# Eight-bit product stage without GpSimd: VectorE adds the bias, TensorE the residual, ScalarE copies the sum to x

## The chip, the cores and the metric

The kernel runs on one core of one Trainium2 chip. The core has a matrix engine (TensorE, PE in the profile), a vector engine (VectorE, DVE), a scalar engine (ScalarE, ACT), GpSimd (POOL), and SyncE (SP), which issues most of the transfers. Each engine takes its own instructions in order and waits on semaphores. The metric is the device time of one execution in microseconds.

## The reference, cut to what matters

The program is eight stages on x (4096 tokens of 128 values): four attentions and four feed-forward parts, each `x = x + f(layernorm(x))`. The change touches the fourth stage alone:

```
x_hat = layernorm(x).astype(bfloat16)
x_q = (x_hat.astype(float32) / s_in).astype(float8_e4m3fn)
k_q = (kernel.astype(float32) / s_k).astype(float8_e4m3fn)
y   = dot(x_q, k_q) * (s_in * s_k)          # 128 x 128 product in float32
x   = x + (y.astype(bfloat16) + bias)       # bias is bfloat16
```

## The kernel before, in words

x stays in SBUF for the whole program as 32 tiles of 128 tokens x 128 values. The eight-bit stage, `fp8_product`, treats them as 8 units of 4 tiles (`UNITS = 8`, `UNIT = 4`), so a unit is a 128x512 block. It lies at about 793 to 847 us of the profiled execution, between the attention `attn1` and the attention `attn2`; `end_of_stage` puts a barrier of all engines between stages.

The steps of a unit u, each with its line in the kernel before:

- ScalarE `normalise_unit(u)`: four ACTIVATE of one tile each (L1332), then one of 128x512 that divides by the input scale (L1340).
- VectorE `round_unit(u)`: four instructions that round to eight-bit precision (L1272, L1274, L1278, L1280).
- ScalarE `guard_unit(u)` (L1347), then VectorE `quantize_unit(u)` (L1288), which writes x_q.
- TensorE: four transposes of x_q (L1383); ScalarE `take_turned(u)` copies them from PSUM (L1354); TensorE: four products (L1389).
- ScalarE `cast_unit(u)` scales the product and rounds it to bfloat16 as y_bf (L1360).
- GpSimd adds the bias to y_bf (L1315) and then y_biased to x in place (L1319).
- VectorE `stats(u)`: four BATCH_NORM_STATS2 on the new x (L1294), which the layer norm of the next stage needs.

The order on each engine is written out in the code as a software pipeline over slots s. In slot s VectorE does round(s), stats(s-3), quantize(s-1); ScalarE does guard(s), take_turned(s-1), normalise(s+2), cast(s-1); TensorE goes unit by unit, transposes(u) and products(u); GpSimd goes unit by unit. Buffers are pairs, and so a step of unit u may also wait for unit u-2.

Before its last two stats, VectorE calculates the norm constants of the first half of the tiles (`norm_scale(FIRST_HALF)`, L197 to L212: some twenty small dependent instructions). At the end of its work TensorE does 12 `keep_warm` matmuls (L638), whose results nobody reads; the next stage's TensorE code begins with 10 more of these, and only then does it touch its own data (L1047, the first transposes of `attn2`).

Of the kernel before, what the change touches and what calls it, by code (L numbers as in the profile page):

```python
# [22 lines left out]
ALU = mybir.AluOpType  # L23
# [3 lines left out]
P = 128  # L27
# [7 lines left out]
UNIT = 4  # L35
UNITS = TILES // UNIT
# [94 lines left out]
class Core:  # L131
# [15 lines left out]
    def sb(self, name, shape, dt=F32, stack=None):  # L147
        return (stack or self.stack).enter_context(self.nc.sbuf_tensor(name, shape, dt))

    def sem(self, name):  # L150
        return self.stack.enter_context(self.nc.semaphore(name))
# [29 lines left out]
FIRST_HALF, SECOND_HALF = slice(0, HALF_TILES), slice(HALF_TILES, TILES)  # L181
# [73 lines left out]
def arrived(core, eng, *names):  # L255
    for group in names:
        eng.wait_ge(core.loaded[group], core.loads[group])
# [376 lines left out]
def keep_warm(core, bank, n):  # L634

    moving = core.w["minus_huge"][:, 0:8].rearrange("p t k -> p (t k)")
    for _ in range(n):
        core.nc.tensor.matmul(bank[:], core.w["route_lower"][:], moving, start=True, stop=True)  # L638
# [582 lines left out]
def fp8_product(core):  # L1221

    nc, w = core.nc, core.w
    with ExitStack() as stack:
        sb = lambda n, shape, dt=F32: core.sb("fp8_" + n, shape, dt, stack)
        pair = lambda n, shape, dt=F32: [sb(f"{n}{k}", shape, dt) for k in range(2)]
        sem = lambda n: core.stage_sem("fp8_" + n)
# [5 lines left out]
        ident_bf = sb("ident_bf", [P, P], BF16)  # L1233
# [3 lines left out]
        y_bf, y_biased = pair("y_bf", [P, UTOK], BF16), pair("y_biased", [P, UTOK], BF16)  # L1237
# [1 line left out]
        prepared, k_rounding, shifted = sem("prepared"), sem("k_rounding"), sem("shifted")  # L1239
        normed, valued, rounding, guarded, quantized = (sem(n) for n in ("normed", "valued", "rounding", "guarded", "quantized"))  # L1240
        xt_made, xt_taken, made_y, y_cast = sem("xt_made"), sem("xt_taken"), sem("made_y"), sem("y_cast")
        y_summed, added, stats_made = sem("y_summed"), sem("added"), sem("stats_made")
        t_bank, y_bank = core.bank[0:2], core.bank[2:4]
        t_bf = [t_bank[k][:].bitcast(BF16)[:, 0:UTOK] for k in range(2)]
        x_of = lambda u: core.x[:, u * UNIT:(u + 1) * UNIT].rearrange("p a c -> p (a c)")
        ROUND = 4

        with nc.Block() as block:

            @block.vector  # L1250
            def _(dve):
                def shifts(tiles):
                    nc.vector.scalar_tensor_tensor(shift[:, tiles], core.mean[:, tiles], -1.0, core.rstd[:, tiles],
                                                   ALU.mult, ALU.mult).then_inc(shifted, 1)

                shifts(FIRST_HALF)
                arrived(core, dve, "fp8", "ident")
                nc.vector.tensor_copy(ident_bf[:], w["ident"][:])
                nc.vector.tensor_tensor(product[:], w["fp8_scales"][:, 0:1], w["fp8_scales"][:, 1:2], ALU.mult)
                nc.vector.reciprocal(inverses[:], w["fp8_scales"][:]).then_inc(prepared, 1)  # L1260
                dve.wait_ge(prepared, 1)
                nc.vector.tensor_scalar(value[1][:, 0:P], w["fp8_kernel"][:], inverses[:, 1:2], None, ALU.mult).then_inc(prepared, 1)
                dve.wait_ge(prepared, 2)
                quantize(core, dve, k_rounding, lambda n: n, value[1][:, 0:P], (power[:, 0:P], rounded[1][:, 0:P]), kernel_q[:])
                dve.wait_ge(k_rounding, QUANTIZE_STEPS)
                norm_scale(core, dve, SECOND_HALF)
                shifts(SECOND_HALF)

                def round_unit(u):
                    v, r = value[u % 2][:], rounded[u % 2][:]  # L1270
                    dve.wait_ge(valued, u + 1)
                    nc.vector.tensor_scalar(power[:].bitcast(U32), v.bitcast(U32), 0x7F800000, None, ALU.bitwise_and).then_inc(rounding, 1)  # L1272
                    dve.wait_ge(rounding, ROUND * u + 1)
                    nc.vector.tensor_scalar(power[:], power[:], 2.0 ** -6, 1.5 * 2.0 ** 20, ALU.max, ALU.mult).then_inc(rounding, 1)  # L1274
                    dve.wait_ge(rounding, ROUND * u + 2)
                    if u >= 2:
                        dve.wait_ge(quantized, u - 1)
                    nc.vector.tensor_tensor(r, v, power[:], ALU.add).then_inc(rounding, 1)  # L1278
                    dve.wait_ge(rounding, ROUND * u + 3)
                    nc.vector.tensor_tensor(r, r, power[:], ALU.subtract).then_inc(rounding, 1)  # L1280
                    dve.wait_ge(rounding, ROUND * u + 4)

                def quantize_unit(u):
                    dve.wait_ge(guarded, u + 1)
                    if u >= 2:
                        dve.wait_ge(xt_made, u - 1)

                    nc.vector.scalar_tensor_tensor(x_q[u % 2][:], guard[u % 2][:], 0.0, rounded[u % 2][:], ALU.mult, ALU.add  # L1288
                                                   ).then_inc(quantized, 1)

                def stats(u):
                    dve.wait_ge(added, u + 1)
                    for t in range(u * UNIT, (u + 1) * UNIT):
                        ins = nc.vector.bn_stats(core.stats[:, t], core.x[:, t])  # L1294
                    ins.then_inc(stats_made, 1)

                for s in range(UNITS + 3):
                    if s == UNITS + 1:
                        dve.wait_ge(stats_made, UNITS // 2)
                        norm_scale(core, dve, FIRST_HALF)  # L1300
                    if s < UNITS:
                        round_unit(s)
                    if 0 <= s - 3:
                        stats(s - 3)
                    if 0 <= s - 1 < UNITS:
                        quantize_unit(s - 1)

            @block.gpsimd
            def _(pool):
                arrived(core, pool, "fp8")  # L1310
                for u in range(UNITS):
                    pool.wait_ge(y_cast, u + 1)
                    if u >= 2:
                        pool.wait_ge(added, u - 1)
                    nc.gpsimd.tensor_tensor(y_biased[u % 2][:].rearrange("p (t c) -> p t c", t=UNIT),  # L1315
                                            y_bf[u % 2][:].rearrange("p (t c) -> p t c", t=UNIT),
                                            w["fp8_bias"][:].unsqueeze(1).to_broadcast([P, UNIT, P]), ALU.add).then_inc(y_summed, 1)
                    pool.wait_ge(y_summed, u + 1)
                    nc.gpsimd.tensor_tensor(x_of(u), x_of(u), y_biased[u % 2][:], ALU.add).then_inc(added, 1)  # L1319

            @block.scalar
            def _(act):
# [33 lines left out]
                def cast_unit(u):  # L1356
                    act.wait_ge(made_y, u + 1)
                    if u >= 2:
                        act.wait_ge(y_summed, u - 1)
                    nc.scalar.activation(y_bf[u % 2][:], y_bank[u % 2][:], ACT.Copy, scale=product[:, 0:1]).then_inc(y_cast, 1)  # L1360

                act.wait_ge(prepared, 1)
                normalise_unit(0)
                normalise_unit(1)
                for s in range(UNITS + 2):
                    if s < UNITS:
                        guard_unit(s)
                    if 0 <= s - 1 < UNITS:
                        take_turned(s - 1)
                    if s + 2 < UNITS:  # L1370
                        normalise_unit(s + 2)
                    if 0 <= s - 1 < UNITS:
                        cast_unit(s - 1)

            @block.tensor
            def _(pe):
                pe.wait_ge(k_rounding, QUANTIZE_STEPS)
                for u in range(UNITS):
                    pe.wait_ge(quantized, u + 1)
                    if u >= 2:  # L1380
                        pe.wait_ge(xt_taken, u - 1)
                    for t in range(UNIT):
                        ins = nc.tensor.transpose(t_bf[u % 2][:, t * P:t * P + P], x_q[u % 2][:, t * P:t * P + P], ident_bf[:])  # L1383
                    ins.then_inc(xt_made, 1)
                    pe.wait_ge(xt_taken, u + 1)
                    if u >= 2:
                        pe.wait_ge(y_cast, u - 1)
                    for t in range(UNIT):
                        ins = nc.tensor.matmul(y_bank[u % 2][:, t * P:t * P + P], x_qt[u % 2][:, t * P:t * P + P], kernel_q[:],  # L1389
                                               start=True, stop=True)  # L1390
                    ins.then_inc(made_y, 1)
                arrived(core, pe, "route")
                keep_warm(core, core.bank[4], 12)


def unit_stats(core, dve, added, u):
# [1978 lines left out]
```

## Time and profile before

| what | value |
|---|---|
| median of 3 runs | 1744.29 us (1738.72 to 1745.17) |
| profiled execution: its own time | 1731.64 us |
| profiled execution: span of its instructions | 1729.8 us |
| mean granted TensorE clock over the span | 0.903 |
| busy over the span: PE, PEld, DVE, ACT, POOL | 1373.9, 1141.8, 1048.9, 920.8, 624.5 us |

The shares of the whole program say little on this stage: it takes about 54 us of 1730, and what bounds it has to be read from its own stretch. A row of a timeline gives start, duration, engine, line, operation and tiles; several equal instructions in a row are merged with xN. In brackets stands how long the engine was idle before, and who released it.

### The profile page before, as it was taken

The numbers are of one execution on the slowest core, as the hardware profiler recorded it, in microseconds if no ns is written. First come the engines' busy times: TensorE is split into PE (matmuls) and PEld (weight loads), VectorE is DVE, ScalarE is ACT, GpSimd is POOL, SyncE is SP. The second block draws the span as 40 slices with busy tenths as digits, with TensorE's granted clock in tenths as the row PEclk, the third lists the DMA queues.
The fourth block names the chain that finished last, engine by engine and source line by source line (L and its number), as shares of the span: only waits on it lengthen the run. The fifth ranks groups of instructions, "written<-read, shape, count | busy, mean of one in ns | idle before, by whom it ended". The sixth has DMA issues, their size and how long they took to land. (4 is left out here: it accounts for less than half of the span.)

```text
span 1729.8 us, 43197 instructions
## 1 busy us (share of the span) xinstructions
PE 1373.9 (79%) x16821; PEld 1141.8 (66%) x16821; DVE 1048.9 (61%) x2733; ACT 920.8 (53%) x2096; POOL 624.5 (36%) x604
## 2 busy tenths in 40 slices
PE   4799999978999998993588757777728878669893
PEld 3688888756788895872256536667725766559893
DVE  5677777753444327997899966333357878633334
ACT  2466656543454446986355325444456766326664
POOL 2332333230000003331478604777722245444442
PEclk9899999988999999995699969899968988679997
DMA  9200000029990002310000010111130000112225
GB/s 304 54 18 18 18 19 17 2 62 146 177 132 1 1 1 74 115 59 1 16 17 20 2 49 28 47 44 46 45 114 25 14 30 24 32 43 72 66 62 163
DMA packets 143529, 94.12 MB, mean 54 GB/s; under 512 B 55776, under 2 KB 130272, under 8 KB 142816
## 3 DMA queue, kind: packets, MB, share of 16 engines
q1 hardware_dynamic: 134368, 72.86, 19.6%
q0 software_dynamic: 8960, 18.50, 3.4%
q8 instruction: 136, 2.23, 0.6%
q14 instruction: 65, 0.53, 0.1%
HBM read 51.20 MB, written 40.12 MB: 53 GB/s over the span
## 5 line engine op out<-in xcount | busy, mean ns | idle before, releaser
L399 POOL TENSOR_TENSOR wide_probs<-wide_probs,wide_key_mask 128x512 f32<-128x512 f32 x64 | 82.9, 1316 | 187.2 <-ACT wide_probs L520 187.2
L1759 ACT ACTIVATE moe_hidden<-bank,moe_staged 128x128 f32<-128x128 f32 x288 | 82.2, 369 | 79.2 <-PE bank L1853 55.1
L1864 PE MATMUL bank<-moe_staged,moe_hidden 128*128 128x128 f32 x576 | 85.2, 294 | 37.2 <-ACT moe_hidden L1759 25.7
L1535 POOL DMA_INDIRECT moe_x_rows<-moe_rows,moe_source x72 | 81.3, 1129 | 77.5 <-DVE moe_source L1631 55.8
L2595 DVE TENSOR_TENSOR moe_hidden<-bank,moe_gate 128x256 f32<-128x256 f32 x104 | 44.1, 424 | 105.3 <-ACT moe_gate L2681 84.4
L1864 PEld LDWEIGHTS bank<-moe_staged,moe_hidden 128*128 128x128 f32 x576 | 75.2, 204 | 43.1 <-ACT moe_hidden L1759 29.2
L2585 POOL DMA_INDIRECT moe_results<-moe_y_rows,moe_x_rows x72 | 68.9, 958 | 90.1 <-DVE moe_y_rows L2607 65.7
L738 POOL MEMSET attn_v_bd<- 128x576 f32 x2 | 1.1, 578 | 267.6 <-POOLq L162 267.6
L768 POOL TENSOR_TENSOR attn_col_bd<-attn_col_t,group_mask_sb 128x1024 f32<-128x1024 f32 x32 | 60.7, 1898 | 86.9 <-ACT attn_row_t L969 86.9
L1541 POOL DMA_INDIRECT moe_results<-moe_y_rows,moe_dest x72 | 79.6, 1106 | 33.9 <-issue 19.0
L998 ACT ACTIVATE attn_probs<-attn_probs 128x1024 f32<-128x1024 f32 x64 | 64.2, 1049 | 50.0 <-DVE attn_probs L872 49.6
L844 DVE TENSOR_REDUCE attn_top<-bank 128x8 f32<-128x512 f32 x128 | 79.3, 682 | 18.3 <-PE bank L1030 18.3
L3029 ACT ACTIVATE moe_router<-bank,moe_rb_sb 128x512 f32<-128x512 f32 x64 | 41.4, 688 | 91.5 <-PE bank L3133 67.4
L1853 PE MATMUL bank<-moe_xb_t,moe_staged 128*128 128x128 f32 x576 | 83.5, 292 | 2.1 <-issue 1.5
L1674 DVE TENSOR_TENSOR moe_y_rows<-bank,moe_staged 128x128 f32<-128x128 f32 x72 | 20.9, 291 | 105.1 <-remote 65.0
L2731 PE MATMUL bank<-moe_xb_t,moe_staged 128*128 128x128 f32 x576 | 79.3, 281 | 0.8 <-ACT moe_xb_t L2675 0.5
L1853 PEld LDWEIGHTS bank<-moe_xb_t,moe_staged 128*128 128x128 f32 x576 | 76.1, 206 | 4.7 <-ACT moe_xb_t L1745 2.5
L872 DVE TENSOR_TENSOR attn_probs<-bank,attn_top 128x512 f32<-128x512 f32 x128 | 78.3, 675 | 0.0
L1647 DVE COPY moe_staged<-moe_pack_sb 128x1156 f32 x72 | 57.0, 793 | 31.5 <-DVE moe_y_rows L1674 18.7
L1913 POOL DMA_INDIRECT moe_rows<-moe_xhat,moe_slot x64 | 62.1, 970 | 35.9 <-issue 15.9
L2731 PEld LDWEIGHTS bank<-moe_xb_t,moe_staged 128*128 128x128 f32 x576 | 69.8, 191 | 5.1 <-ACT moe_xb_t L2675 4.7
L2681 ACT ACTIVATE moe_gate<-bank 128x256 f32<-128x256 f32 x104 | 39.8, 385 | 57.2 <-PE bank L2731 52.4
(416 smaller groups left out, 4265.2 us busy)
## 6 DMA issues: line engine op xcount, KB each, us to landing
moe_rows<-route_empty_sb SPq DMA_DIRECT2D x8, 2624.0 KB, 22.7
attn_ctx<-in_ctx_t SPq DMA_DIRECT2D x48, 128.0 KB, 2.0
moe_x_rows<-moe_rows SPq DMA_DIRECT2D x72, 66.0 KB
moe_pack_sb<-in_moe_pack SPq DMA_DIRECT2D x8, 578.0 KB, 3.9
moe_w_sb<-in_moe_w SPq DMA_DIRECT2D x2, 2048.0 KB, 10.7
moe_hot<-moe_results SPq DMA_DIRECT2D x16, 256.0 KB, 6.2
moe_y_in<-moe_results SPq DMA_DIRECT2D x16, 256.0 KB, 6.0
moe_pack_sb<-in_moe_pack SPq DMA_DIRECT2D x9, 384.0 KB, 4.3
```

Of the source, the lines that this page charges most:

```text
L399: nc.gpsimd.tensor_tensor(probs[b.parity][:, :, h2], probs[b.parity][:, :, h2], keys, ALU.mult).then_inc(masked, 1)
L844: nc.vector.tensor_reduce(top[:, j], s_bank[j][:].rearrange("p (n k) -> p n k", k=SEQ), AX, ALU.max).then_inc(topped, 1)
L872: ins = nc.vector.tensor_tensor(probs[b.parity][:, :, 4 * j:4 * j + 4], s_bank[j][:].rearrange("p (t g k) -> p t g k", t=2, k=SEQ), top[:, ...
L998: nc.scalar.activation(part, part, ACT.Exp, scale=scale).then_inc(exped, 1)
L1535: nc.gpsimd.indirect_dma_start(x_rows[s % GATHERS][:], None, rows, bass.IndirectOffsetOnAxis(ap=source[:, s:s + 1], axis=0)).then_inc(gath ...
L1541: nc.gpsimd.indirect_dma_start(results, bass.IndirectOffsetOnAxis(ap=dest[:, b:b + 1], axis=0), y_rows[b % GATHERS][:], None).then_inc(sca ...
L1759: ins = nc.scalar.activation(hidden[m % 2][:, f], hid_bank[m % 2][:, f * P:(f + 1) * P], ACT.Gelu, bias=staged[b % STAGED][:, b1_at + f:b1 ...
L1853: ins = nc.tensor.matmul(bank[m % 2][:, at:at + P], weights[:, k * P:(k + 1) * P], rhs, start=True, stop=True)
L1864: ins = nc.tensor.matmul(y_bank[m % 2][:, 0:P], hidden[m % 2][:, f], weights[:, at:at + P], start=(f == 0), stop=(f == nf - 1))
L1913: nc.gpsimd.indirect_dma_start(core.rows, bass.IndirectOffsetOnAxis(ap=self.slot[:, k, at:at + 1], axis=0), self.xhat[:, at], None).then_i ...
L2585: nc.gpsimd.indirect_dma_start(results, bass.IndirectOffsetOnAxis(ap=x_rows[b % LOADS][:, P:P + 1].bitcast(U32), axis=0), y_rows[b % GATHE ...
L2731: ins = nc.tensor.matmul(bank[m % 2][:, at:at + P], weights[:, k * P:(k + 1) * P], rhs, start=True, stop=True)
```

## The change

GpSimd has no work left in the stage. Its bias addition goes to VectorE (`bias_unit`, the same 128x512 bfloat16 operation), in slot s for unit s-2, between round(s) and stats(s-3). The residual addition goes to TensorE (`add_unit`): an identity product of x (float32, 512 columns) and an identity product of y_biased (bfloat16, 512 columns), accumulated in one of two PSUM banks. ScalarE copies the sum from PSUM to x (`take_sum`), in slot s for unit s-2, behind cast(s-1). `norm_scale(FIRST_HALF)` moves from ahead of slot 9 to the end of slot 8, and the 12 keep_warm matmuls write another bank.

```diff
@@ vector
+                def bias_unit(u):
+                    dve.wait_ge(y_cast, u + 1)
+                    if u >= 2:
+                        dve.wait_ge(summed, u - 1)
+                    nc.vector.tensor_tensor(y_biased[u % 2][:].rearrange("p (t c) -> p t c", t=UNIT),
+                                            y_bf[u % 2][:].rearrange("p (t c) -> p t c", t=UNIT),
+                                            w["fp8_bias"][:].unsqueeze(1).to_broadcast([P, UNIT, P]), ALU.add).then_inc(y_summed, 1)
+
                 for s in range(UNITS + 3):
-                    if s == UNITS + 1:
-                        dve.wait_ge(stats_made, UNITS // 2)
-                        norm_scale(core, dve, FIRST_HALF)
                     if s < UNITS:
                         round_unit(s)
+                    if 0 <= s - 2 < UNITS:
+                        bias_unit(s - 2)
                     if 0 <= s - 3:
                         stats(s - 3)
                     if 0 <= s - 1 < UNITS:
                         quantize_unit(s - 1)
-
-            @block.gpsimd
-            def _(pool):
-                arrived(core, pool, "fp8")
-                for u in range(UNITS):
-                    pool.wait_ge(y_cast, u + 1)
-                    if u >= 2:
-                        pool.wait_ge(added, u - 1)
-                    nc.gpsimd.tensor_tensor(y_biased[u % 2][:].rearrange("p (t c) -> p t c", t=UNIT),
-                                            y_bf[u % 2][:].rearrange("p (t c) -> p t c", t=UNIT),
-                                            w["fp8_bias"][:].unsqueeze(1).to_broadcast([P, UNIT, P]), ALU.add).then_inc(y_summed, 1)
-                    pool.wait_ge(y_summed, u + 1)
-                    nc.gpsimd.tensor_tensor(x_of(u), x_of(u), y_biased[u % 2][:], ALU.add).then_inc(added, 1)
+                    if s == UNITS:
+                        dve.wait_ge(stats_made, UNITS // 2)
+                        norm_scale(core, dve, FIRST_HALF)
@@ scalar
+                def take_sum(u):
+                    act.wait_ge(summed, u + 1)
+                    nc.scalar.copy(x_of(u), sum_bank[u % 2][:]).then_inc(added, 1)
+
-                for s in range(UNITS + 2):
+                for s in range(UNITS + 3):
 ...
                     if 0 <= s - 1 < UNITS:
                         cast_unit(s - 1)
+                    if 0 <= s - 2 < UNITS:
+                        take_sum(s - 2)
@@ tensor
+                def add_unit(u):
+                    pe.wait_ge(y_summed, u + 1)
+                    if u >= 2:
+                        pe.wait_ge(added, u - 1)
+                    nc.tensor.matmul(sum_bank[u % 2][:], w["ident"][:], x_of(u), start=True, stop=False)
+                    nc.tensor.matmul(sum_bank[u % 2][:], ident_bf[:], y_biased[u % 2][:], start=False, stop=True).then_inc(summed, 1)
 ...
                     ins.then_inc(made_y, 1)
+                    if u >= 1:
+                        add_unit(u - 1)
+                add_unit(UNITS - 1)
                 arrived(core, pe, "route")
-                keep_warm(core, core.bank[4], 12)
+                keep_warm(core, core.bank[6], 12)
```

The order on VectorE in a middle slot, before (round, stats, quantize; the lines are those of the kernel before):

```order
793 L1272 TENSOR_SCALAR fp_power<-fp_value 128x512
794 L1274 TENSOR_SCALAR fp_power<-fp_power 128x512
795 L1278 TENSOR_TENSOR fp_rounded<-fp_value,fp_power 128x512
796 L1280 TENSOR_TENSOR fp_rounded<-fp_rounded,fp_power 128x512
797 L1294 BN_STATS stats<-x 128x6 x4
798 L1288 SCALAR_TENSOR_TENSOR fp_x_q<-fp_guard,fp_rounded 128x512
```

And with the change (L1295 is `bias_unit`):

```order
796 L1272 TENSOR_SCALAR fp_power<-fp_value 128x512
797 L1274 TENSOR_SCALAR fp_power<-fp_power 128x512
798 L1278 TENSOR_TENSOR fp_rounded<-fp_value,fp_power 128x512
799 L1280 TENSOR_TENSOR fp_rounded<-fp_rounded,fp_power 128x512
800 L1295 TENSOR_TENSOR fp_y_biased<-fp_y_bf,fp_bias_sb 128x512
801 L1302 BN_STATS stats<-x 128x6 x4
802 L1288 SCALAR_TENSOR_TENSOR fp_x_q<-fp_guard,fp_rounded 128x512
```

The bias addition stands ahead of stats and quantize, so that both are queued behind its wait for y_bf.

The order on ScalarE in a middle slot with the change (guard, take_turned, normalise of two instructions' kinds, cast, take_sum; all but the last, L1361, stood in this order before):

```order
465 L1344 ACTIVATE fp_guard<-fp_rounded 128x512
466 L1351 COPY fp_x_qt<-bank 128x512
467 L1329 ACTIVATE fp_x_bf<-x,fp_shift,rstd 128x128 x4
468 L1337 ACTIVATE fp_value<-fp_x_bf,fp_inverses 128x512
469 L1357 ACTIVATE fp_y_bf<-bank,fp_product 128x512
470 L1361 COPY x<-bank 128x512
```

The cast stands behind the whole normalise, as it did before.

The order on TensorE of a unit with the change (transposes, products, and the two identity products of the unit ahead of it; before only the first two rows of each unit were there):

```order
1644 L1395 MATMUL bank<-fp_ident_bf,fp_x_q 128x128 x4
1645 L1401 MATMUL bank<-fp_kernel_q,fp_x_qt 128x128 x4
1646 L1387 MATMUL bank<-x,ident_sb 128x512
1647 L1388 MATMUL bank<-fp_y_biased,fp_ident_bf 128x512
```

The addition of unit u-1 is queued behind the products of unit u.

## Rows read from the trace of the kernel before

**Rows 1.** Timeline of VectorE in the stage and behind it (start, duration, instruction).
```profile
804.29 0.69 DVE L1288 SCALAR_TENSOR_TENSOR fp_x_q<-fp_guard,fp_rounded 128x512 bf16<-128x512 f32 x1
804.90 0.42 DVE L1272 TENSOR_SCALAR fp_power<-fp_value 128x512 uint32<-128x512 uint32 x1
...
807.26 0.69 DVE L1288 SCALAR_TENSOR_TENSOR fp_x_q<-fp_guard,fp_rounded 128x512 bf16<-128x512 f32 x1
...
818.09 0.87 DVE L1294 BATCH_NORM_STATS2 stats<-x 128x6 f32<-128x128 f32 x4
818.88 0.67 DVE L1288 SCALAR_TENSOR_TENSOR fp_x_q<-fp_guard,fp_rounded 128x512 bf16<-128x512 f32 x1
819.47 1.37 DVE L1272 TENSOR_SCALAR fp_power<-fp_value 128x512 uint32<-128x512 uint32 x1
...
837.33 0.67 DVE L1288 SCALAR_TENSOR_TENSOR fp_x_q<-fp_guard,fp_rounded 128x512 bf16<-128x512 f32 x1
...
845.06 1.65 DVE L1294 BATCH_NORM_STATS2 stats<-x 128x6 f32<-128x128 f32 x8
...
849.85 0.17 DVE L197 TENSOR_TENSOR mean<-stats 128x16 f32<-128x16 f32 x1
...
853.20 0.18 DVE L212 SCALAR_TENSOR_TENSOR rstd<-norm_half,rstd 128x16 f32<-128x16 f32 x1
```

**Rows 2.** All engines over the stretch of the stage (busy, instructions, granted clock).
```profile
799.00:847.00 48.00, 13.57 (x76) 7.10 (x76) 45.29 (x95) 27.37 (x54) 21.00 (x16) 0.54 0.00 1
```

**Rows 3.** Timeline of GpSimd around one stretched VectorE instruction.
```profile
819.08 1.47 POOL L1315 TENSOR_TENSOR fp_y_biased<-fp_y_bf,fp_bias_sb 128x512 bf16<-128x512 bf16 x1 [3.23 <-ACT fp_y_bf L1360]
```

**Rows 4.** Timeline of ScalarE, unit 0's cast and one whole slot.
```profile
808.54 0.67 ACT L1360 ACTIVATE fp_y_bf<-bank,fp_product 128x512 bf16<-128x512 f32 x1
...
815.55 0.58 ACT L1354 COPY fp_x_qt<-bank 128x512 bf16<-128x512 bf16 x1 [1.96 <-PE bank L1383]
816.03 1.65 ACT L1332 ACTIVATE fp_x_bf<-x,fp_shift,rstd 128x128 bf16<-128x128 f32 x4
817.71 0.72 ACT L1340 ACTIVATE fp_value<-fp_x_bf,fp_inverses 128x512 f32<-128x512 bf16 x1
818.34 0.67 ACT L1360 ACTIVATE fp_y_bf<-bank,fp_product 128x512 bf16<-128x512 f32 x1
```

**Rows 5.** ScalarE copying 128x512 float32 from PSUM in the stage before.
```profile
788.70 0.58 ACT L959 COPY attn_probs_t<-bank 128x512 f32<-128x512 f32 x1 [0.27 <-PE bank L1059]
```

**Rows 6.** Timeline of TensorE in the stage and at the next one's start.
```profile
814.90 0.61 PE L1383 MATMUL bank<-fp_ident_bf,fp_x_q 128*128 128x128 bf16 x4 [4.04 <-DVE fp_x_q L1288]
...
839.83 0.61 PE L1389 MATMUL bank<-fp_kernel_q,fp_x_qt 128*128 128x128 bf16 x4 [0.83 <-ACT fp_x_qt L1354]
840.23 4.25 PE L638 MATMUL bank<-minus_huge,route_lower_sb 128*128 128x512 bf16 x12
847.68 4.43 PE L638 MATMUL bank<-minus_huge,route_lower_sb 128*128 128x512 bf16 x10 [3.20 <-PEq L162]
851.90 0.63 PE L1047 MATMUL bank<-ident_sb,attn_xhat 128*128 128x128 f32 x2
...
859.30 0.70 PE L1086 MATMUL bank<-attn_x_t,attn_wq_sb 128*128 128x256 f32 x2 [0.46 <-ACT attn_x_t L947]
859.83 0.59 PE L1087 MATMUL bank<-attn_ctx,attn_wk_sb 128*128 128x256 f32 x2
```

**Rows 7.** TensorE alone by stretches: busy, granted clock (0.50 is half).
```profile
800.00:840.00 40.00, 9.09 (x62) 0.50 0.00 1
840.00:845.00 5.00, 4.48 (x16) 0.68 0.00 0
845.00:850.00 5.00, 2.32 (x6) 0.67 0.25 75
```

**Rows 8.** A bfloat16 TENSOR_TENSOR on VectorE elsewhere: duration ns min/median/max.
```profile
L1618 DVE TENSOR_TENSOR moe_hot<-route_iota_sb,moe_split x8: 1215/1217/1218, 1032.3 to 1046.8; 128x1024 bf16<-128x1024 bf16 x8
```

More of the change, by code:

```diff
@@ L1241, in fp8_product @@
         xt_made, xt_taken, made_y, y_cast = sem("xt_made"), sem("xt_taken"), sem("made_y"), sem("y_cast")
-        y_summed, added, stats_made = sem("y_summed"), sem("added"), sem("stats_made")
-        t_bank, y_bank = core.bank[0:2], core.bank[2:4]
+        y_summed, summed, added, stats_made = sem("y_summed"), sem("summed"), sem("added"), sem("stats_made")
+        t_bank, y_bank, sum_bank = core.bank[0:2], core.bank[2:4], core.bank[4:6]
         t_bf = [t_bank[k][:].bitcast(BF16)[:, 0:UTOK] for k in range(2)]
@@ L1373, in _ @@
                         cast_unit(s - 1)
+                    if 0 <= s - 2 < UNITS:
+                        take_sum(s - 2)
             @block.tensor
             def _(pe):
+                arrived(core, pe, "ident")
                 pe.wait_ge(k_rounding, QUANTIZE_STEPS)
+                def add_unit(u):
[4 more added lines that the diff above has]
+                    nc.tensor.matmul(sum_bank[u % 2][:], ident_bf[:], y_biased[u % 2][:], start=False, stop=True).then_inc(summed, 1)
                 for u in range(UNITS):
```

## The prediction, made before the changed kernel ran

> **What bounds the stage now.** I read the stage's own stretch first, then the timelines of its engines side by side. Over 799 to 847 us VectorE is busy 45.29 of 48 us and GpSimd 21.00 [rows 2], so VectorE sets the pace, and GpSimd's work is hidden beside it. The reader should then look at VectorE's durations. A unit of rounding starts at 804.90 and its quantize at 807.26 [rows 1]: 2.36 us for four instructions while GpSimd is idle. The same L1272 takes 1.37 us at 819.47 in place of 0.42, while GpSimd does its bias addition at 819.08 to 820.55 [rows 1, 3]. Two things on VectorE are not stretched: the four statistics (0.87 us) and a quantize that meets no GpSimd work (0.67 us). The pace of before: the first quantize ends at 804.98, the last (of eight) at 838.00, so 7 steps in 33.02 us, 4.72 each; in the middle, where GpSimd works in each unit, about 5.3. TensorE is busy 9.09 of 40 us at half clock [rows 7] and ScalarE has waits of about 2 us in a slot [rows 4].
>
> **What the change removes.** GpSimd's 16 instructions lie beside VectorE's work, so their own time counts only at the tail, and what disappears is the stretching of VectorE. Without it a slot of VectorE would cost, start to start: rounding 2.36, statistics 0.79 (818.09 to 818.88), quantize 0.59 (818.88 to 819.47) [rows 1]. The bias addition is new on VectorE. The nearest row of the same length is the quantize at 807.26, 0.69 us for 128x512 from two tensors to bfloat16 [rows 1]; the nearest bfloat16 row, L1618, takes 1.217 us for 1024 elements, which is the same price per element [rows 8]. I take 0.69 (0.60 start to start); half of the elements' part, 0.42, is the lower bound, by L1272's row of a faster form of the same length. The sum is 4.34 us, less than 4.72. If VectorE never waited, the stage would be shorter.
>
> The Trainium skill (VectorE: DVE Perf Modes, "The perf-mode tier table") says that a tensor_tensor whose tensors are all bfloat16 runs at two elements a cycle; L1618's row [rows 8] shows one, though its second operand is spread along the innermost dimension and the bias is not. By the page the addition would take about 0.42 us by estimate, by the row 0.69. It is behind a wait and beside a longer path in all slots but the first, so the sum would differ by 0.3 us.
>
> **What it adds: a wait in front of quantize.** The bias addition of unit s-1 comes in slot s+1, right behind rounding, and waits for ScalarE's cast of the same unit; statistics and quantize are queued behind it. I follow one slot from T, the end of quantize(s-1), with durations and gaps of [rows 1, 4, 6]:
>
> - TensorE's transposes start at T+0.06 and end at T+0.67 (814.90, 0.61).
> - ScalarE's take_turned runs T+0.71 to 1.29, and normalise begins 0.48 behind its start; from there to the start of the cast it is 2.31 us (816.03 to 818.34), so the cast starts at T+3.50 and ends at T+4.17.
> - VectorE has ended its rounding at T+2.3 and stands still for 1.9 us. The bias addition runs T+4.21 to 4.90.
> - The statistics wait for take_sum(s-2), which ScalarE does behind that cast, from T+4.07 at the earliest. It needs the sum from TensorE. The products start at T+1.35, and the next matmul can start 0.40 later (839.83 to 840.23), at T+1.75. At full clock a 256-column float32 product (two rows in the trace) takes 0.53 us until the next starts (859.30 to 859.83). Twice the columns at half the clock is at most 4 x 0.53 = 2.12, where the loading of the weights, which does not grow with the columns, is counted twice too often. The lower end is 4 times a bfloat16 product of 512 columns (4.22 us for ten keep_warm at half clock, 0.42 each), 1.69, since 0.53 for 256 columns is 5 times that product's price per column, loading included. I take 1.9. The bfloat16 product adds 0.63 until its result is there (its own streaming 0.43, drain 0.2). The sum is ready at T+1.75+1.9+0.63 = T+4.28.
> - take_sum, at L959's 0.58 [rows 5], runs T+4.32 to 4.90 (0.67 as the cast would be the upper bound). Statistics start at T+4.94, quantize at T+5.73, and it ends at T+6.42.
>
> So the step is 6.42 us where it was 4.72. It is a loop through four engines: ScalarE's normalise lies between the transposes and the cast, which nobody on VectorE was waiting for until now. The bounds of it are 6.3 (sum and copy early, only cast and bias) and 6.7 (2.12 and 0.67). For the last two steps there is no normalise, but the sum is still at T+4.28 in TensorE's queue, and the step stays 6.42 at half clock.
>
> The walk from the start: quantize(0) ends at 804.98 as before. Slot 2 has no statistics, so quantize(1) waits only for the cast of unit 0 (ends 809.21 [rows 4]) and the addition: 809.25+0.60+0.69 = 810.54. Six more steps of 6.42 give 849.1 for the end of quantize(7), against 838.0: 11.1 us later.
>
> **The tail.** Before, 8.7 us pass from there to VectorE's last statistics (845.06+1.65 = 846.71), some of it stretched norm_scale. After: norm_scale takes 3.5 us as at 849.85 to 853.38 [rows 1], the bias of unit 7 ends at T+4.2, its sum at T+6.65, its copy at T+7.3, its statistics at T+8.2. TensorE however has its 12 keep_warm behind the last sum. Before they were done at 844.5, under VectorE's cover; now they start near T+6.4. TensorE is then busy without a break since T+1.35, and before the clock had risen within 3.4 us of such work (mean 0.68 in 840 to 845 [rows 7]). With the rise near T+6.5 the 12 take 2.7 us and end at T+9.2 (8.4 to 10.1 for a rise from T+4.8 to T+8.2). The stage ends at 849.1+9.2 = 858.3 against 846.7: +11.6.
>
> **Given back in the next stage.** There TensorE starts with ten keep_warm in 4.22 us (847.68 to 851.90 [rows 6]) at half clock, after 3.2 us idle. The x_hat of attn2 was ready about 3 us before they ended, so their time is on the path. After the change the idle gap is about 1 us, the clock should still be up, and the ten take 2.1: minus 2.1 us.
>
> The sum is +11.6 - 2.1 = +9.5 us on the profiled execution's own 1731.64 us, so 1741.1. The median of the runs shown lies 12.65 above that execution; nothing in the change touches what lies between, so I put the same +9.5 on the median: 1744.29+9.5 = 1753.8 us. A measurement of this kernel can tell about 0.5%, 8.7 us, from no change; the forecast lies just beyond.
>
> **Rivals.**
>
> *A. The loop does not close: VectorE's own work sets the pace.* If the cast came no later than T+2.3, the step would be 4.34, quantize(7) would end at 804.98+7x4.34 = 835.4, the stage at 844.6, and with the gain in attn2 it is -4.2: 1740.1. For it: VectorE is 94% busy before and loses its stretching. Against: the order on ScalarE puts 2.31 us of normalise ahead of the cast [rows 4]; the point from which it decides is a cast ending 1.9 us earlier.
>
> *B. The new products raise TensorE's clock.* They make 3 us of work in each 6.4 where it was 1.2. At full clock the sum of the last two steps is there at T+3.1 and the steps take 5.2, which saves 2.4; in the tail sum and keep_warm are shorter, the stage ends at T+8.0. +11.1-2.4-0.7-2.1 = +5.9: 1750.2. In the earlier steps the cast is as late as before, so that only 0.1 each is had. For it: the clock rose in 840 to 845; against: it stayed at 0.50 for 800 to 840 with the short bursts of before, and each unit leaves a gap of over 3 us.
>
> *C. Nothing is given back.* The clock has fallen by the time attn2 starts, or the float32 product and the copy have their upper prices (6 x 0.3 = 1.8 us): +11.3 to +11.6, 1755.8. For it: the clock fell between 845 and 850 in the trace of before [rows 7].
>
> **How the numbers follow.** Forecast 0.50, A 0.06, B 0.18, C 0.20, others 0.06 (of both signs). The clock of the attention stages behind also falls otherwise when they start at another time; attn2 has stretches at half clock, and a shift of 2 to 3 us either way can come from that, about as much as the runs differ (6.5 us). Range: 1745 to 1761, which leaves out A and both far ends. Slower by over 0.5%: a good half of the forecast (0.28), most of C (0.16), a little of B and the others (0.07): 0.51. Faster by over 0.5% (-8.7 us): even A does not reach it without luck in the clock, which with a part of the others gives 0.05. The rest, 0.44, is within 0.5%.
>
> **What would show it.** The step: VectorE idle about 1.9 us ahead of L1295 (`bias_unit`), released by ScalarE's y_bf, in each middle slot, and about 6.4 us from quantize to quantize. No stretched VectorE instruction; L1272 at 0.42 throughout. The float32 identity product as two rows of about 1.05 us at half clock. Quantize(7) ending near 849, the keep_warm near 858, and the ten keep_warm of attn2 in about 2.1 us. The prediction is wrong if VectorE has no wait ahead of L1295, or if the stage ends before 852.

## The result and the profile after

The changed kernel takes 1748.78 us (median of 20 runs, 1740.30 to 1758.73) against 1741.10 us (20 runs, 1732.45 to 1745.48) for the kernel before: a ratio of 1.0044, 95% interval 1.0027 to 1.0061. It is slower by 7.7 us, clear of noise, and just within 0.5%. The forecast was 9.5 us, put on 1744.29, the median of three runs; those three lie 3.2 us above the median of all 20, and so 3.2 of the 5.0 us between 1753.8 and 1748.78 come from where the sum was put.

VectorE in a middle slot of the changed kernel, as a timeline (start, duration, instruction, idle time before it and who ended it); it answers to [rows 1]:

```profile
816.65 0.68 DVE L1288 SCALAR_TENSOR_TENSOR fp_x_q<-fp_guard,fp_rounded 128x512 bf16<-128x512 f32 x1
817.24 0.42 DVE L1272 TENSOR_SCALAR fp_power<-fp_value 128x512 uint32<-128x512 uint32 x1
...
818.88 0.69 DVE L1280 TENSOR_TENSOR fp_rounded<-fp_rounded,fp_power 128x512 f32<-128x512 f32 x1
821.57 0.43 DVE L1295 TENSOR_TENSOR fp_y_biased<-fp_y_bf,fp_bias_sb 128x512 bf16<-128x512 bf16 x1 [2.00 <-PE bank L1388]
822.17 0.87 DVE L1302 BATCH_NORM_STATS2 stats<-x 128x6 f32<-128x128 f32 x4 [0.17 <-ACT x L1361]
822.96 0.67 DVE L1288 SCALAR_TENSOR_TENSOR fp_x_q<-fp_guard,fp_rounded 128x512 bf16<-128x512 f32 x1
```

L1272 takes 0.42 us, where a row of before had 1.37: the stretching is gone. In its place VectorE stands still for 2.0 us ahead of the bias addition. Ahead of it the row names TensorE's L1388, but by the code this addition (unit 2) waits for a sum of unit 0, which was long there. Of the two waits it has, ScalarE's y_bf of unit 2 is the late one, as ScalarE's timeline shows; it answers to [rows 4]:

```profile
818.03 0.58 ACT L1351 COPY fp_x_qt<-bank 128x512 bf16<-128x512 bf16 x1 [1.67 <-PE bank L1395]
818.51 1.65 ACT L1329 ACTIVATE fp_x_bf<-x,fp_shift,rstd 128x128 bf16<-128x128 f32 x4
820.19 0.72 ACT L1337 ACTIVATE fp_value<-fp_x_bf,fp_inverses 128x512 f32<-128x512 bf16 x1
820.82 0.67 ACT L1357 ACTIVATE fp_y_bf<-bank,fp_product 128x512 bf16<-128x512 f32 x1
821.55 0.58 ACT L1361 COPY x<-bank 128x512 f32<-128x512 f32 x1
822.03 0.63 ACT L1344 ACTIVATE fp_guard<-fp_rounded 128x512 f32<-128x512 f32 x1
```

The cast ends at 821.49, the bias addition starts at 821.57. The copy ends at 822.13 and the statistics start at 822.17. TensorE in the same slot, then at the end of the stage, answers to [rows 6]:

```profile
818.67 0.61 PE L1401 MATMUL bank<-fp_kernel_q,fp_x_qt 128*128 128x128 bf16 x4 [0.68 <-ACT fp_x_qt L1351]
819.07 2.02 PE L1387 MATMUL bank<-x,ident_sb 128*128 128x512 f32 x2
820.88 0.63 PE L1388 MATMUL bank<-fp_y_biased,fp_ident_bf 128*128 128x512 bf16 x1
...
852.84 1.59 PE L1387 MATMUL bank<-x,ident_sb 128*128 128x512 f32 x2 [0.32 <-DVE fp_y_biased L1295]
854.27 0.38 PE L1388 MATMUL bank<-fp_y_biased,fp_ident_bf 128*128 128x512 bf16 x1
854.48 2.75 PE L638 MATMUL bank<-minus_huge,route_lower_sb 128*128 128x512 bf16 x12
858.17 2.32 PE L638 MATMUL bank<-minus_huge,route_lower_sb 128*128 128x512 bf16 x10 [0.94 <-PEq L162]
860.53 0.41 PE L1047 MATMUL bank<-ident_sb,attn_xhat 128*128 128x128 f32 x2
```

The float32 product costs 1.81 us until the next can start. The 12 keep_warm end at 857.23, when VectorE has been done since 856.17, and the ten of the next stage take 2.36 us, where they took 4.22. TensorE's granted clock by single microseconds answers to [rows 7] (length, busy with the number of instructions, clock; the last two figures are of the DMA):

```profile
846.00:847.00 1.00, 0.33 (x1) 0.50 0.00 0
847.00:848.00 1.00, 0.00 (x0) 1.00 0.00 0
...
850.00:851.00 1.00, 1.00 (x5) 0.70 0.00 0
...
853.00:854.00 1.00, 1.00 (x2) 0.59 0.00 0
```

It stayed at half from 800 to 847, went up for some 4 us while TensorE was idle, fell back in 850 to 851, and rose again at about 853.8, in the tail.

Three lengths are compared from here on, all read from profiles: from the end of quantize(0) to that of quantize(7); from the stage's first VectorE instruction to the next stage's; and from there on to attn2's first L844 (the first maximum of its scores).

| kernel | quantize(0) to (7) | stage | stage and on to attn2's first L844 |
|---|---|---|---|
| before | 33.0 | 54.3 | 65.3 |
| changed | 43.2 | 64.0 | 72.8 |

The last column differs by 7.5 us, close to the measured 7.7. The spans of the two profiles differ by 10.8, with 0.7 of it ahead of the stage and 2.6 behind. One profile's span is no measure of the change: in the six profiled on one chip the stage begins between 790.6 and 797.4 us, though all that lies ahead of it is the same, and what follows the first L844 takes 816.4 to 823.5 us.

### The profile page after: what moved, and what is told of

It reads as the page before. It is cut to its first block and busy times, and to the rows that moved or that the text cites. A ratio compares the mean times of both kernels' runs of the same rounds, so it can differ in the third digit from the quotient of the medians.

```text
span 1740.6 us, 43220 instructions
## 1 busy us (share of the span) xinstructions
PE 1387.5 (80%) x16820; PEld 1150.0 (66%) x16845; DVE 1043.5 (60%) x2741; ACT 924.6 (53%) x2104; POOL 599.5 (34%) x588
## 5 line engine op out<-in xcount | busy, mean ns | idle before, releaser
L1879 PEld LDWEIGHTS bank<-moe_staged,moe_hidden 128*128 128x128 f32 x576 | 79.1, 213 | 39.2 <-ACT moe_hidden L1774 26.1
L2610 DVE TENSOR_TENSOR moe_hidden<-bank,moe_gate 128x256 f32<-128x256 f32 x104 | 44.1, 424 | 99.1 <-ACT moe_gate L2696 78.2
L1868 PE MATMUL bank<-moe_xb_t,moe_staged 128*128 128x128 f32 x576 | 86.9, 300 | 7.0 <-ACT moe_xb_t L1760 5.1
L844 DVE TENSOR_REDUCE attn_top<-bank 128x8 f32<-128x512 f32 x128 | 79.2, 680 | 19.5 <-PE bank L1030 19.5
L2746 PE MATMUL bank<-moe_xb_t,moe_staged 128*128 128x128 f32 x576 | 79.5, 281 | 1.4 <-ACT moe_xb_t L2690 0.7
## 6 DMA issues: line engine op xcount, KB each, us to landing
moe_w_sb<-in_moe_w SPq DMA_DIRECT2D x2, 2048.0 KB, 10.8
```

The lines of the kernel that those rows point to most:

```text
L844: nc.vector.tensor_reduce(top[:, j], s_bank[j][:].rearrange("p (n k) -> p n k", k=SEQ), AX, ALU.max).then_inc(topped, 1)
L1868: ins = nc.tensor.matmul(bank[m % 2][:, at:at + P], weights[:, k * P:(k + 1) * P], rhs, start=True, stop=True)
L1879: ins = nc.tensor.matmul(y_bank[m % 2][:, 0:P], hidden[m % 2][:, f], weights[:, at:at + P], start=(f == 0), stop=(f == nf - 1))
L2746: ins = nc.tensor.matmul(bank[m % 2][:, at:at + P], weights[:, k * P:(k + 1) * P], rhs, start=True, stop=True)
```

## The experiments

They ran in four groups on three chips; each ratio is against the kernel before, run beside it in the same group. Its median was 1679.23, 1682.31, 1676.13 and 1732.15 us. Repeats of one kernel in two groups differ by up to 0.2%, about 3 us, so less than that is read from profiles alone.

**Everything one slot later.** Bias addition, identity products and copy for unit s-3, statistics for unit s-4; the loops of VectorE and ScalarE run one slot longer, and `add_unit(UNITS - 2)` is added behind TensorE's loop.

```diff
-                    if 0 <= s - 2 < UNITS:
-                        bias_unit(s - 2)
-                    if 0 <= s - 3:
-                        stats(s - 3)
+                    if 0 <= s - 3 < UNITS:
+                        bias_unit(s - 3)
+                    if 0 <= s - 4:
+                        stats(s - 4)
...
-                        take_sum(s - 2)
+                        take_sum(s - 3)
...
-                    if u >= 1:
-                        add_unit(u - 1)
+                    if u >= 2:
+                        add_unit(u - 2)
```

> The changed kernel with the bias addition, the identity products and the copy one slot later (units s-3), and the statistics one more (s-4). Theory (the loop through ScalarE's cast sets the step): nothing waits for a cast of the same round, the step from quantize to quantize falls from 6.31 to about 4.5 us, which is ScalarE's own work in a slot; quantize(7) comes about 13 us earlier than in the changed kernel, the tail grows by 1 to 2 us, and the whole is about 11 us faster than the changed kernel, 3 to 5 us faster than before. Rival 1 (TensorE's float32 product at half clock sets the step): the step stays near 6.3. Rival 2 (VectorE's added work): no change either.

Measured: 1.0017 of before (0.9999 to 1.0035), middle steps of 6.3 us, quantize(0) to (7) in 38.8, stage 61.5. The theory as I had put it was wrong by one wait. VectorE's timeline in this kernel:

```profile
824.29 0.42 DVE L1295 TENSOR_TENSOR fp_y_biased<-fp_y_bf,fp_bias_sb 128x512 bf16<-128x512 bf16 x1
826.85 0.87 DVE L1302 BATCH_NORM_STATS2 stats<-x 128x6 f32<-128x128 f32 x4 [2.13 <-ACT x L1361]
827.64 0.68 DVE L1288 SCALAR_TENSOR_TENSOR fp_x_q<-fp_guard,fp_rounded 128x512 bf16<-128x512 f32 x1
```

The bias addition waits for nothing now, and the statistics wait 2.13 us. I had moved copy and statistics together, so that the statistics of a slot still wait for the last instruction of ScalarE's slot before, and quantize stands behind them. Whether the cast or TensorE's sum holds the copy, this run does not tell: the first steps take 3.0 and 4.1 us, but they lie ahead of the first float32 product as well as of the first copy, and later both are equally late (the cast ends at 826.16, the sum at 826.19, the copy starts at 826.23). In the last step, where no normalise delays the cast, it is the sum, and that step still takes 6.29 us.

**Only the statistics one slot later.** One line of that edit alone, in the changed kernel; VectorE's loop runs one slot longer.

```diff
-                    if 0 <= s - 3:
-                        stats(s - 3)
+                    if 0 <= s - 4:
+                        stats(s - 4)
```

> The changed kernel with only the statistics one slot later (s-4). Theory: the wait for the cast stays and the wait for the copy goes: middle steps 6.05 in place of 6.31 us; the last two steps, where no normalise lies ahead of the cast, 4.5 in place of 6.31. Together about 4.6 us faster than the changed kernel. Rival (the cast alone counts, the sum on TensorE never): the last two steps stay at 6.3 and the gain is 1 us. Rival (the sum and its copy are what counts throughout): all steps near 4.5, 11 us.

Measured: 1.0012 (0.9992 to 1.0033). Middle steps 6.05 us, the last two 4.56 and 4.52, quantize(0) to (7) 37.7 in place of 43.2; the stage and on to the first L844, 66.7 in place of 72.8. The last two quantize of this kernel, and below them ScalarE's copy in one of the last slots of the changed kernel, which waits for the sum:

```profile
834.90 0.67 DVE L1288 SCALAR_TENSOR_TENSOR fp_x_q<-fp_guard,fp_rounded 128x512 bf16<-128x512 f32 x1
839.41 0.68 DVE L1288 SCALAR_TENSOR_TENSOR fp_x_q<-fp_guard,fp_rounded 128x512 bf16<-128x512 f32 x1
```

```profile
840.49 0.58 ACT L1361 COPY x<-bank 128x512 f32<-128x512 f32 x1 [1.55 <-PE bank L1388]
```

So each of the two waits alone holds the step near 6.1 to 6.3, the cast because normalise lies ahead of it; where no normalise does, only the sum and its copy held it. The profile's gain is 6 us, more than the 4.6 expected: 5.5 us lie in the steps, since the second one, in whose slot no statistics stand any more, fell to 5.28 us, and a later one to 5.83 with the clock up; 0.5 us lie in the tail.

**The cast ahead of normalise.**

```diff
-                    if s + 2 < UNITS:
-                        normalise_unit(s + 2)
                     if 0 <= s - 1 < UNITS:
                         cast_unit(s - 1)
+                    if s + 2 < UNITS:
+                        normalise_unit(s + 2)
```

> The changed kernel with ScalarE's cast ahead of normalise in each slot. Theory (two waits, the cast and the copy of the sum, which now lies behind normalise): the bias addition comes 1.5 us earlier, but the statistics wait longer, middle steps 7.0 us in place of 6.31, the first step 3.7 in place of 5.3, the whole within 2 us of the changed kernel. Rival (only the place of the cast counts): steps near 4.8, 6 to 8 us faster than the changed kernel.

Measured: 1.0056 (1.0033 to 1.0080), first step 3.88, middle steps 6.93, 45.1 in all.

```profile
823.65 0.43 DVE L1295 TENSOR_TENSOR fp_y_biased<-fp_y_bf,fp_bias_sb 128x512 bf16<-128x512 bf16 x1 [0.52 <-ACT fp_y_bf L1357]
826.35 0.87 DVE L1302 BATCH_NORM_STATS2 stats<-x 128x6 f32<-128x128 f32 x4 [2.28 <-ACT x L1361]
```

The wait for the cast shrinks to 0.52 us and the wait for the copy takes its place and more. The place of the cast alone is not the cause.

**Without the 12 keep_warm.** The two lines `arrived(core, pe, "route")` and `keep_warm(core, core.bank[6], 12)` are taken out.

> The changed kernel without the 12 keep_warm matmuls at the end of the stage. Theory (they outlast VectorE's last statistics by 1.1 us, but keep the clock up for the next stage): the stage ends 1.1 us earlier and the ten keep_warm of the next take 4.2 us in place of 2.3; about 1 us slower in all. Rival (they keep nothing up): 1.1 us faster, the ten still in 2.3 us.

Measured: 1.0075 (1.0050 to 1.0100, 6 runs). The profile agrees with the theory in the stage: it ends 1.0 us earlier, TensorE is idle for 2.48 us, and the ten take 3.84 us.

```profile
856.28 0.38 PE L1388 MATMUL bank<-fp_y_biased,fp_ident_bf 128*128 128x512 bf16 x1
859.15 4.00 PE L638 MATMUL bank<-minus_huge,route_lower_sb 128*128 128x512 bf16 x10 [2.48 <-PEq L162]
862.99 0.38 PE L1047 MATMUL bank<-ident_sb,attn_xhat 128*128 128x128 f32 x2
```

On to the first L844 that is 73.2 us, 0.4 more than with them. The time is 5 us above the changed kernel's ratio, with intervals that overlap; what the rest would be is open.

**GpSimd's work cut to one column.** In the kernel before, both additions work on 1 of 512 columns (the second is shown, the first is cut in the same way); most of bias and product is not added to x.

```diff
...
-                    nc.gpsimd.tensor_tensor(x_of(u), x_of(u), y_biased[u % 2][:], ALU.add).then_inc(added, 1)
+                    nc.gpsimd.tensor_tensor(x_of(u)[:, 0:1], x_of(u)[:, 0:1], y_biased[u % 2][:, 0:1], ALU.add).then_inc(added, 1)
```

> The kernel before with GpSimd's two additions cut to one column of 512 each (most of the bias and the product is not added to x). Theory (VectorE's instructions are stretched only while GpSimd reads and writes): no VectorE instruction of the stage is stretched, the steps fall from 4.72 to about 3.95 us, quantize(7) comes 6.3 us earlier, the tail is 2 us shorter, and with the clock still up in the next stage the whole is 8 to 10 us faster than before. Rival (the stretching has another cause): L1272 still takes up to 1.37 us, and the time is within 1 us of before.

Measured: 0.9922 (0.9894 to 0.9950), steps 3.87, 24.5 us in all, stage 44.3. L1272 over its eight instructions (duration ns min/median/max):

```profile
L1272 DVE TENSOR_SCALAR fp_power<-fp_value x8: 419/427/428, 803.7 to 828.3; 128x512 uint32<-128x512 uint32 x8
```

GpSimd's reads and writes are what stretched VectorE: without them it is 8.5 us less between the first and last quantize (6.3 were expected), and 10 over the stage.

**20 keep_warm in the kernel before.** `keep_warm(core, core.bank[4], 12)` becomes `keep_warm(core, core.bank[4], 20)`; run twice.

> The kernel before with 20 in place of 12 keep_warm matmuls at the end of the stage. Theory (the time given back in the next stage of the changed kernel is the clock alone): TensorE ends its 20 about 0.5 us before VectorE ends the stage, so the stage costs the same; the clock is still up when the next stage starts and its ten take 2.3 us in place of 4.4: 2.1 us faster than before. Rival (the gain in the next stage comes from something else): no change, the ten still 4.4 us.

> The kernel before with 20 keep_warm matmuls once more. Theory: 2.3 us of the next stage, 0.14% faster than before. Rival (the first measurement's 0.3%): 5 us faster.

Measured: 0.9969 (0.9953 to 0.9985) and 0.9987 (0.9965 to 1.0009). The profile:

```profile
839.41 5.80 PE L638 MATMUL bank<-minus_huge,route_lower_sb 128*128 128x512 bf16 x20
846.68 2.32 PE L638 MATMUL bank<-minus_huge,route_lower_sb 128*128 128x512 bf16 x10 [1.48 <-PEq L162]
```

The stage is as long as before (54.1), and on to the first L844 it is 62.8, which is 2.5 us less. So what the change gives back in the next stage is the clock, and it was to be had without the change. By time the two runs give 0.3% and 0.1%, the second not clear of none; the 2.5 us are the profile's.

**Quantize first in the changed kernel.** One move on VectorE; run twice.

```diff
+                    if 0 <= s - 1 < UNITS:
+                        quantize_unit(s - 1)
                     if 0 <= s - 2 < UNITS:
                         bias_unit(s - 2)
                     if 0 <= s - 3:
                         stats(s - 3)
-                    if 0 <= s - 1 < UNITS:
-                        quantize_unit(s - 1)
```

> The changed kernel with one edit of order on VectorE: in each slot quantize(s-1) stands ahead of bias(s-2) and stats(s-3), not behind them. Theory (the step is long because quantize is queued behind two waits, for the cast and for the copy, both of ScalarE's slot before): both waits leave the loop, and ScalarE's own slot of about 4.5 us (take_turned 0.48, normalise 2.31, cast 0.73, copy 0.48, guard 0.5) sets the step. From quantize(0) to quantize(7) 30 us in place of 43.2, 11 to 13 us faster than the changed kernel, and with the clock still up in the next stage 3 to 6 us faster than before. Rival (a longer chain over TensorE, a shift by whole slots as in the kernel with everything one slot later): steps stay near 6.3.

> Quantize ahead of bias and statistics once more. Theory (the stage is 12 us shorter than the changed kernel's and 2 shorter than before's, and the next starts 2.3 us faster): 0.7% faster than the changed kernel, 0.2% faster than before. Rival (what the stage saves is lost behind it): not faster than before, 0.3% faster than the changed kernel.

Measured: middle steps of 4.5 us, quantize(0) to (7) in 27.7 in place of 43.2, with all of the added work still there. TensorE's clock rose in this kernel, but only at about 821.1; the step from 815.48 to 820.01 took 4.53 us with the float32 product at half clock:

```profile
814.79 0.69 DVE L1288 SCALAR_TENSOR_TENSOR fp_x_q<-fp_guard,fp_rounded 128x512 bf16<-128x512 f32 x1
817.61 2.02 PE L1387 MATMUL bank<-x,ident_sb 128*128 128x512 f32 x2
819.32 0.69 DVE L1288 SCALAR_TENSOR_TENSOR fp_x_q<-fp_guard,fp_rounded 128x512 bf16<-128x512 f32 x1
```

ScalarE, whose rows show no wait from 811.0 to 826.0, now sets the step. The times: 1.0015 (0.9993 to 1.0036) and 0.9994 (0.9971 to 1.0017), no faster than before, where 3 to 6 us less had been expected at first; beside the second run the changed kernel took 7.3 us more. Part of the 15.5 us is lost in the tail, which grew from 9.2 to 12.8 us:

```profile
833.88 0.38 PE L1388 MATMUL bank<-fp_y_biased,fp_ident_bf 128*128 128x512 bf16 x1
837.03 1.12 PE L1387 MATMUL bank<-x,ident_sb 128*128 128x512 f32 x2 [2.78 <-DVE fp_y_biased L1295]
838.00 0.47 PE L1388 MATMUL bank<-fp_y_biased,fp_ident_bf 128*128 128x512 bf16 x1
838.26 4.39 PE L638 MATMUL bank<-minus_huge,route_lower_sb 128*128 128x512 bf16 x12
```

TensorE waits for the last bias addition behind norm_scale, and the clock falls. By the profile it is 61.1 us from the stage's start to the first L844, 4.2 less than before; that the times show none of it is not explained by this stage.

**The same order in the kernel before, with 20 keep_warm.** Quantize stands ahead of the statistics.

> The kernel before with 20 keep_warm matmuls and quantize ahead of the statistics. Theory (VectorE's own stretched work sets the step of before, no wait): the order changes nothing, 33 us from quantize(0) to quantize(7), and the whole is as the one with 20 keep_warm alone, 0.3% faster than before. Rival (the statistics' wait for GpSimd costs time before too): 1 to 3 us faster than that.

Measured: 0.9999 (0.9971 to 1.0026); 30.5 us in place of the 33.0 expected, stage 52.6. The expectation that the order changes nothing was wrong in the profile: it is worth 2.5 us between the quantize and 1.5 in the stage. It was not the rival's wait either, since VectorE's rows of before show a single wait between the first and the last quantize, 0.71 us for ScalarE's normalise, and none for GpSimd. The middle steps are 4.8, since VectorE's work is still stretched, but less often, as its instructions now meet GpSimd's elsewhere; and about 1 us of VectorE's work moves behind the last quantize. To the first L844 0.6 us are left of it (62.2 against 62.8 with 20 keep_warm alone). The time shows none of it.

**Quantize first, and norm_scale behind the last bias addition.** The edit against the kernel with quantize first:

```diff
                     if 0 <= s - 2 < UNITS:
                         bias_unit(s - 2)
+                    if s == UNITS + 1:
+                        dve.wait_ge(stats_made, UNITS // 2)
+                        norm_scale(core, dve, FIRST_HALF)
                     if 0 <= s - 3:
                         stats(s - 3)
-                    if s == UNITS:
-                        dve.wait_ge(stats_made, UNITS // 2)
-                        norm_scale(core, dve, FIRST_HALF)
```

> Quantize first, and norm_scale moved from ahead of the last bias addition to right behind it. In the kernel with quantize first alone TensorE waited 2.8 us for that addition behind norm_scale, its clock fell, and its 12 keep_warm took 4.4 us. Theory: the last identity products start about 2.5 us earlier, the 12 take 2.7 us, and the stage ends 2.5 to 3 us earlier than with quantize first alone; 0.15% faster than it and 0.4% faster than before. Rival: VectorE's last statistics come no earlier, no gain.

> The changed kernel once more, beside the others of this call on one chip, since the differences between calls are as large as what is looked for. Theory: 0.4% slower than before, as on the first chip; 43.2 us from quantize(0) to quantize(7). Rival (the chip decides): within 0.1% of before.

Measured side by side: this kernel 0.9958 (0.9940 to 0.9976), the changed kernel 1.0046 (1.0027 to 1.0066), with 43.2 us from quantize(0) to (7) once more. The stage is 50.2 us, and on to the first L844 it is 59.0. The end on TensorE:

```profile
838.84 0.63 PE L1388 MATMUL bank<-fp_y_biased,fp_ident_bf 128*128 128x512 bf16 x1
839.27 1.91 PE L1387 MATMUL bank<-x,ident_sb 128*128 128x512 f32 x2
840.97 0.53 PE L1388 MATMUL bank<-fp_y_biased,fp_ident_bf 128*128 128x512 bf16 x1
841.34 2.75 PE L638 MATMUL bank<-minus_huge,route_lower_sb 128*128 128x512 bf16 x12
```

No wait is left between the last two sums. The stage is 2.0 us shorter than with quantize first alone, where 2.5 to 3 were expected. The division of work of the change, in another order, beats the kernel before by 0.4% and the changed kernel by 0.9%. Against the kernel before with 20 keep_warm, run beside it (1732.46 us), it is 6.7 us faster, though the two intervals just touch; norm_scale moved in the kernel before was not run.

## Why the prediction was right

- *The step.* Forecast 6.42 us, a loop from quantize over TensorE, ScalarE's normalise and cast, the bias and the statistics. Measured 6.31, with 2.0 us of waiting ahead of L1295 where 1.9 were forecast. That it is this loop, and not the added work, is shown by the order alone: 4.5 us with quantize first, the clock at half in both. The float32 product was put at 1.9 and took 1.81.
- *Two waits, not one.* The working had both, the cast (T+4.17) and the copy (T+4.90), but the first test of it took only one out and still expected the gain. The runs with each wait taken out alone (6.3 and 6.05) show that they are nearly equal.
- *The bias addition.* 0.69 us was taken from the rows, and 0.42 was measured, the lower bound. The Trainium skill's rule (VectorE: DVE Perf Modes, "The perf-mode tier table") holds: all bfloat16, two elements a cycle, 0.425 us for 512. The row that I preferred, L1618, was not its equal, having an operand spread along the innermost dimension. It was worth 0.3 us, in the first step; in the others the addition is behind a longer path.
- *Quantize(0) to (7).* Forecast 44.1, measured 43.2: 0.3 from the bias, the rest from the product.
- *The tail.* Forecast T+9.2, measured T+8.4, the early end of the bounds given: the clock rose at about T+5.0, where T+6.5 had been assumed and T+4.8 was the bound. Why it rose that early no run shows. The keep_warm did outlast VectorE, by 1.1 us.
- *Given back.* Forecast 2.1 us, all of it in the ten keep_warm, measured 2.3 (from 11.0 to 8.7 us from the start of attn2 to its first L844), of which the ten give 1.9; shown apart from the change with 20 keep_warm.
- Rival B, the clock, came in for a part: it rose, but too late for the steps. The time alone does not decide between the two, as +7.7 lies midway between the forecast's +9.5 and B's +5.9; the last two steps do, at 6.30 and 6.31 us where B had 5.2. Rival A, where the loop does not close, is nearly what the better order made true (4.5 us by ScalarE, where A had 4.34 by VectorE).

In all 10.2 us later at quantize(7), 0.4 us back in the tail, 2.3 in the next stage: +7.5 by the profile. The forecast was +11.1, +0.5 in the tail and -2.1, so +9.5. No term was off by more than 1 us, but all three were off the same way.

## What to carry to other kernels

When work moves to an engine that takes its instructions in order, price the waits that come with it and count what is queued behind each, not only the durations. Here a slot had 0.6 us less work on the busiest engine (4.1 us by the rows of the changed kernel, where a step had been 4.72) and became 1.6 us longer, and putting the one instruction that starts the next round ahead of those that finish the last round took both waits out of the loop. A wait is out only when no other instruction of the same slot waits for the same place on the other engine: shifting producer and consumer together leaves it.

## What was not expected of the hardware

GpSimd's instructions of 1.2 to 1.6 us lengthened VectorE's by up to 0.95 us, for the one-tensor instructions (L1272, 0.42 to 1.37) by more than their own duration, and left the statistics alone (0.87 us with and without). Rows of the kernel before:

```profile
810.64 1.48 POOL L1319 TENSOR_TENSOR x<-x,fp_y_biased 128x512 f32<-128x512 f32 x1
811.14 1.52 DVE L1280 TENSOR_TENSOR fp_rounded<-fp_rounded,fp_power 128x512 f32<-128x512 f32 x1
...
820.63 1.21 POOL L1319 TENSOR_TENSOR x<-x,fp_y_biased 128x512 f32<-128x512 f32 x1
820.88 1.26 DVE L1274 TENSOR_SCALAR fp_power<-fp_power 128x512 f32<-128x512 f32 x1
...
823.62 0.87 DVE L1294 BATCH_NORM_STATS2 stats<-x 128x6 f32<-128x128 f32 x4
823.79 1.15 POOL L1315 TENSOR_TENSOR fp_y_biased<-fp_y_bf,fp_bias_sb 128x512 bf16<-128x512 bf16 x1 [1.94 <-ACT fp_y_bf L1360]
```

The ends tell more than the lengths. L1274 ends 0.30 us behind GpSimd's L1319 (822.14 and 821.84), L1272 of [rows 1] 0.29 behind the L1315 of [rows 3] (820.84 and 820.55), and the two-tensor L1280, 0.69 us when alone, 0.54 behind its L1319 (812.66 and 812.12). That looks as if the stretched instruction could do its own work only when GpSimd's was through. So it costs what is left of GpSimd's instruction, and not a share of the speed.

TensorE's clock was granted at full for about 4 us from 847. Until then it had been busy for 3.0 to 3.5 us of each slot of 6.3 us, in bursts, at half clock, and it was idle just then; in the five equal slots before, the clock had stayed at half.
